# Fused cross-attention and FFN kernel: GpSimd marks the lower limit of the ternary FFN weights, VectorE sums every other load, limits are worked out one load ahead

## The reference

```
def _bitlinear(x, w_latent):
    scale = clip(mean(abs(w_latent), axis=1), 1e-05)        # one per row
    tern = clip(round(w_latent / scale), -1.0, 1.0)
    return x @ (tern * scale).T
h = _bitlinear(x, w_fc) + gate * (x @ v.T @ fast_b.T @ u.T)  # w_fc 2048 x 512
r = relu(h)
return _bitlinear(r * r, w_proj)                             # w_proj 512 x 2048
```

## Time and profile before

| | before |
|---|---|
| median of three runs | 2805.3 us |
| the profiled execution, span | 2803.6 us |
| the profiled execution's own time | not listed apart from the three runs; the median less the span is 1.7 us |
| attention phase | 0 to about 1651 us |
| preparation of the weights | about 1653 to 1724.7 us |
| batch loop of the FFN | 1724.7 us to the end |

### The profile page before, as it was taken

How to read it: one execution, slowest core, us unless ns; L and a number is a source line. 1 busy time by engine, 2 the same in 40 slices (tenths; PEclk the granted TensorE clock), 3 DMA queues, 4 the chain that set the end, 5 groups by cost and what they waited for, 6 DMA issues and landing times. The chain is left out here.

```text
span 2803.6 us, 46166 instructions
## 1 busy us (share of the span) xinstructions
PE 2666.3 (95%) x15410; PEld 1979.3 (71%) x15410; DVE 1688.5 (60%) x3278; ACT 1111.7 (40%) x1965; POOL 377.6 (13%) x791
## 2 busy tenths in 40 slices
PE   7999999999999999999999967999999999999998
PEld 5666666667666666666766645888888888888887
DVE  4676766776767677677676666444444444444444
ACT  2533443443353344244335245444344334433332
POOL 1212121121121212112112110000000000000000
PEclk9999999999999999999999977999999999999999
DMA  4343253333334325333333332000000000000000
GB/s 129 84 112 99 61 135 92 81 98 98 88 85 114 97 62 134 90 79 103 98 85 88 96 104 76 30 30 30 30 30 30 30 30 30 30 30 30 30 30 31
DMA packets 116803, 198.81 MB, mean 71 GB/s; under 512 B 19987, under 2 KB 22035, under 8 KB 116260
## 3 DMA queue, kind: packets, MB, share of 16 engines
q1 hardware_dynamic: 116772, 198.42, 25.6%
HBM read 63.08 MB, written 33.55 MB: 34 GB/s over the span
## 5 line engine op out<-in xcount | busy, mean ns | idle before, releaser
L715 ACT ACTIVATE probs<-bank 128x512 f32<-128x512 f32 x640 | 369.2, 597 | 339.6 <-PE bank L529 329.6
L1125 PE MATMUL y_bank<-projT,a_hi 128*128 128x512 f32 x1024 | 409.1, 399 | 0.0
L1113 PE MATMUL h_bank<-x2T_hi,fcT 128*128 128x512 f32 x1024 | 406.2, 397 | 0.9 <-ACT scale_row L1196 0.9
L1114 PE MATMUL h_bank<-x2T_lo,fcT 128*128 128x512 f32 x1024 | 406.6, 397 | 0.0
L1127 PE MATMUL y_bank<-projT,a_lo 128*128 128x512 f32 x1024 | 403.9, 394 | 0.0
L1204 ACT ACTIVATE relu<-h_bank,scale_fc 128x512 f32<-128x512 f32 x256 | 176.0, 687 | 464.8 <-PE h_bank L1117 464.8
L464 POOL TENSOR_SCALAR_AFFINE_SELECT probs<-probs 128x256 f32<-128x256 f32 (+1 forms) x640 | 234.1, 366 | 872.7 <-ACT probs L715 870.1
L1314 DVE CAST a_hi<-act_sq 128x512 fp32r<-128x512 f32 x256 | 121.0, 472 | 373.6 <-ACT act_sq L1209 373.6
L529 PE MATMUL bank<-stack 98*128 98x512 f32 (+3 forms) x1024 | 286.0, 351 | 28.3 <-ACT probs L715 26.0
L504 PE MATMUL bank<-stack 96*128 96x512 f32 (+3 forms) x1024 | 266.0, 330 | 17.8 <-DVE maxima L777 11.8
L777 DVE TENSOR_REDUCE maxima<-bank 128x1 f32<-128x512 f32 x256 | 175.9, 687 | 162.2 <-PE bank L508 162.2
(11 more groups left out here) (182 smaller groups left out, 4623.9 us busy)
## 6 DMA issues: line engine op xcount, KB each, us to landing
stack<-stage SPq DMA_DIRECT2D x768, 128.0 KB, 2.3
x_in<-in_x_dram SPq DMA_DIRECT2D x16, 1024.0 KB, 5.3
x<-x_res SPq DMA_DIRECT2D x64, 256.0 KB, 2.4
x_in_sb<-x SPq DMA_DIRECT2D x16, 1024.0 KB, 5.6
out_dram<-y_sb SPq DMA_DIRECT2D x64, 256.0 KB, 2.0
xc_rows<-in_ctx_dram SPq DMA_DIRECT2D x15, 1024.0 KB, 5.2
stack<-m_stage SPq DMA_DIRECT2D x128, 8.0 KB, 1.8
w_nat<-in_L_ffn_w_fc_dram SPq DMA_DIRECT2D x2, 1024.0 KB, 6.7
```

The source lines that it names most:

```text
L715: act.activation(probs[:, s[2], :], t_bank[u % 2][:, :], ACT.Exp, scale=SCALE).then_inc(exp_done, 1)
L1113: pe.matmul(h_bank[b % 2][:, :], fcT[:, k, cols], xT_hi[:, k, :], start=k == 0, stop=False)
L1114: pe.matmul(h_bank[b % 2][:, :], fcT[:, k, cols], xT_lo[:, k, :], start=False, stop=False)
L1125: pe.matmul(y_bank[j][:, :], a_hi[:, b % RING, P * j:P * j + P], projT[:, b, :], start=b == 0, stop=False)
```

## The change

- The mark `neg` moves from VectorE to GpSimd, as one `tensor_scalar` per piece, in order of the pieces. It waits for the limits of its load (a new semaphore `limits_ready`) and for `tern` of piece q-2. VectorE's `tern` of a piece waits for its mark (`neg_ready`).
- ScalarE sums the rows of the even loads only. For an odd load VectorE makes the four sums of absolute values in one `tensor_reduce` over 128 x 2048 elements, after waiting for the load itself.
- `SUMS_AHEAD` goes from 6 to 8.
- The thresholds of load n+1 stand between the two pairs of load n, those of load 0 ahead of the loop.

```
+            for q in range(len(PIECES)):            # GpSimd
+                if q % 4 == 0:
+                    pool.wait_ge(limits_ready, q // 4 + 1)
+                if q >= 2:
+                    pool.wait_ge(tern_ready, q - 1)
+                col = q if q < NB else NB + (q - NB) // CHUNKS
+                pool.tensor_scalar(neg[:, q % 2, :], piece_rows(q), neg_half[:, col:col + 1], None, ALU.is_lt
+                                   ).then_inc(neg_ready, 1)
...
             def row_sum(q):                          # ScalarE
+                if q // 4 % 2 == 1:
+                    return
...
                 if q >= 2:
-                    act.wait_ge(sums_ready, q - 1)
+                    act.wait_ge(sums_ready, 4 * (q // 8) + min(q % 8, 4) - 1)
...
             def thresholds(load):                    # VectorE
-                dve.wait_ge(sums_ready, 4 * load + 4)
+                if load % 2 == 0:
+                    dve.wait_ge(sums_ready, 4 * (load // 2) + 4)
+                else:
+                    dve.wait_ge(wn_loaded[load % 3], load // 3 * 16 + 16)
+                    step(dve.tensor_reduce(parts[:, 4 * load:4 * load + 4], w_rows[load % 3][:, :, :], AX.X, ALU.add,
+                                           apply_absolute_value=True))
...
             def ternary(pair):
-                for q in pair:
-                    ...
-                    self_.inc(dve.tensor_scalar(neg[:, q % 2, :], piece_rows(q), neg_half[:, col:col + 1], None,
-                                                ALU.is_lt))
-                dve.wait_ge(dve_self, self_.now())
                 for q in pair:
                     col = q if q < NB else NB + (q - NB) // CHUNKS
+                    dve.wait_ge(neg_ready, q + 1)
                     if q >= 2:
                         dve.wait_ge(tern_full, q - 1)
                     dve.scalar_tensor_tensor(tern[:, q % 2, :], piece_rows(q), half[:, col:col + 1], neg[:, q % 2, :],
                                              ALU.is_gt, ALU.subtract).then_inc(tern_ready, 1)
...
+            thresholds(0)
             for load in range(len(PIECES) // 4):
-                thresholds(load)
                 ternary((4 * load, 4 * load + 1))
+                if load + 1 < len(PIECES) // 4:
+                    thresholds(load + 1)
                 ternary((4 * load + 2, 4 * load + 3))
```

More of the change, by code:

```diff
@@ L933, in ffn_phase @@
         tern_ready = sem("tern_ready")
+        limits_ready = sem("limits_ready")
+        neg_ready = sem("neg_ready")
         tern_full = sem("tern_full")
@@ L962, in ffn_phase @@
         w_rows = (w_nat, y_sb, x_res)
-        SUMS_AHEAD = 6
+        SUMS_AHEAD = 8
         (PREP_GATE_PE, PREP_GATE_ACT, PREP_A_PE, PREP_A_DVE, PREP_A_HIGH_ACT, PREP_A_LOW_DVE, PREP_U_DVE,
@@ L1241, in thresholds @@
                 self_.inc(dve.tensor_scalar(half[:, cols], scale, 0.5, None, ALU.mult))
-                step(dve.tensor_scalar(neg_half[:, cols], scale, -0.5, None, ALU.mult))
+                dve.tensor_scalar(neg_half[:, cols], scale, -0.5, None, ALU.mult).then_inc(limits_ready, 1)
+                dve.wait_ge(dve_self, self_.now())
             def ternary(pair):
@@ L1246, in ternary @@
                     col = q if q < NB else NB + (q - NB) // CHUNKS
-                    if q >= 2:
-                        dve.wait_ge(tern_ready, q - 1)
-                    self_.inc(dve.tensor_scalar(neg[:, q % 2, :], piece_rows(q), neg_half[:, col:col + 1], None,
-                                                ALU.is_lt))
-                dve.wait_ge(dve_self, self_.now())
-                for q in pair:
-                    col = q if q < NB else NB + (q - NB) // CHUNKS
+                    dve.wait_ge(neg_ready, q + 1)
                     if q >= 2:
```

## The result

The changed kernel takes 2819.44 us (median of four runs, 2815.37 to 2822.84) against 2805.41 for the kernel before; the ratio is 1.0043, with a 95% interval from 1.0029 to 1.0057. It is slower by 0.4%, 12 us by the ratio and 14 by the medians. I had forecast 2808.9 us and a range up to 2814.5, so the measured time lies outside. The direction and the place were right, the size was not.

A forecast was written before the change was run, and what follows sets the result against it. VectorE was taken to bound the weights' preparation, whose end moves with the last `tern`. Moved marks, gaps and stalls saved (-14.1 - 0.5 - 2.6) against reductions, waits and new stalls (+8.8 + 8.0 + 4.0) gave +3.6: 2808.9 us, range 2804 to 2814.5.

The forecast's parts named there:

- Where it bounds, and that the end moves with the last `tern`: In the FFN weights' preparation VectorE is busy 45.68 of 49.5 us; the end moves by what the last `tern` moves.
- The select is the nearest in kind ... I add a fifth and take 0.77: Price of a GpSimd mark: a select's 0.64 us at 512 columns plus a fifth for fetched limit and bf16 narrowing.
- Rival 2: Marks take 0.95 us or more and GpSimd's pairs set the pace: +5.6 at 0.95, +11.7 at 1.29; chance 0.26.
- Taking turns: GpSimd's marks and VectorE's `tern` exclude each other: `tern` holds the way for 0.56 us, a mark for 0.67.
- Reductions: VectorE's four sums of odd loads, 128 x 2048 each, cost 2.2 us apiece, 8.8 us in all.
- Sums eight ahead: ScalarE waits for load 4 before piece 16's sum, delaying copies and transposes: VectorE stalls 4.0 us in place of 2.6.
- my walk: Stepping through the 16 pairs, each start the latest of its engine's last start plus slot, its inputs and the turn.
- The sum: All terms for the preparation: -14.1 - 0.5 - 2.6 + 8.8 + 8.0 + 4.0 = +3.6 us.
- waits on marks: VectorE waits for GpSimd's marks, mostly at first pairs of loads and the last pair: 8.0 us in all.
- Rival 1: `tern` does not take turns with marks: -1.0 us with marks at 0.585, 0.0 at 0.77; chance 0.25.
- Rival 3: Denser transposes raise TensorE's clock earlier for the batch loop's first nine matmuls: at most 1.8 us back; chance 0.03.

The follow-up runs named there:

- idle-marks run: Kernel before plus 32 marks on GpSimd that read the layer-norm input into a spare buffer, nobody waiting: preparation 83.1 us, +11.9 against before.
- Order alone: Kernel before with only the sums eight ahead and the limits one load ahead: preparation 73.7 us, +2.4 against before.
- one mark in four: Kernel before, but GpSimd marks only the fourth piece of each load, into one of four slots: preparation 71.6 us, +0.4 against before.
- rounding: Kernel before with mark and `tern` replaced on VectorE by two one-input passes, through rounded int16: preparation 64.3 us, median 2799.31, ratio 0.9977.

## Why the prediction was wrong

*Where it bounds, and that the end moves with the last `tern`:* right. The last `tern` ends at 1733.87 instead of 1720.95, 12.9 later, and the batch loop starts 12.9 later, its matmuls at 397 ns as before.

*"The select is the nearest in kind ... I add a fifth and take 0.77": this is the step that failed.* A mark takes 1.56 us, twice my value and beyond my upper row, the two-input operation at 1.29. I had let the nearest row by kind of work stand for an instruction with another name, and took a two-input operation for an upper bound, which it isn't for another operation. The runs with a constant limit and an fp32 mark show that my two reasons for the fifth, the limit and the narrowing, are worth 0.08 and nothing.

*Rival 2, marks at 0.95 or more:* this is what happened, and it had 0.26. "GpSimd's pairs set the pace" is in the timeline. But its prices ended at 1.29, and the range already at 1.15.

*Taking turns:* right in kind, wrong in its measure. I let a mark hold the way for nearly all its time (0.67 of 0.77). `tern` loses 0.42 when it starts just behind the start of a mark of 1.56 and nothing when it starts 0.7 into one, and x_low and the reduction lose nothing. By my own prices, from 1.0 (+6.3) to 1.29 (+11.7), a mark of 1.56 would have made some +17 (an estimate, that line drawn on); it came to +12.7, so with the right price the sum would have erred the other way. The Trainium skill (SBUF — State Buffer, Who interferes with whom) has the two engines exclude each other. For which operations collide the runs agree: two SBUF inputs (`tern`) and the fast one-input passes (marks, copies) do, one-input reductions and reads of PSUM don't. In another section of that page (SBUF: two separate sides) the Trainium skill has the loser fully blocked for the whole instruction. On this the runs differ: 0.37 us lost per mark of 1.56 in the idle-marks run, where a copy of 0.585 costs 0.27. Had the rule held for the whole instruction, the pace would have been a mark plus the 0.56 that I let a `tern` hold, 2.1 us per piece; while marks set it, it is 1.54.

*Reductions:* 2.2 each, measured 2.27. Right. *Sums eight ahead:* I had ScalarE standing for 4 us in front of the sum of piece 16, and 4.0 us of stalls on VectorE in place of 2.6. ScalarE does stand, for 3.54. What reaches VectorE is less: in the changed kernel it waits 1.16 for TensorE ahead of `tern` 22, where I had 1.9, and under 0.1 ahead of `tern` 14, where I had 2.1; with the marks back on it, 0.7 in all. Order alone costs the 2.4 us of my walk, but by luck, since most of it is the wait for the sums of load 1. This term was too large.

*The sum:* 8.8 for the reductions and 8.0 for waits on marks. The runs put 7.0 us on reductions and order together, where the terms of my sum without marks on GpSimd (a walk with VectorE's own marks) come to 8.2, and 5.7 on the marks. In my 3.6 the marks were thus a gain of 4.6 us; they are a loss of 5.7. That is 10.3 us of error, less the 1.2 by which the rest was put too high: 9.1, the distance from 3.6 to 12.7. The price of a mark makes it: 32 marks and GpSimd's waits are 61.6 us in a row, where VectorE needed 49.5 for everything, and the marks alone are 50 us (32 x 1.56), where mine were 25 (32 x 0.77). No run has a mark at 0.77; the one with 1.48 shows the direction.

*Rival 1, marks are free:* refuted twice, by idle marks that cost 11.9 us and by one mark in four, which gains nothing. *Rival 3, the clock:* granted 0.58 in the stage against 0.60, and the first matmuls of the batch loop again 0.43 apart. It plays no part in the result. It did come in two other kernels, one mark in four and rounding, whose first matmuls of the batch loop are 0.24 apart at once: the loop is 1.5 us shorter there (1077.4 us against 1078.9 before), near the 1.8 of the rival.

What stays open is what GpSimd does in the 1.56 us, why a mark holds VectorE up behind its start and not later, and why a copy costs VectorE 0.27 and a mark 0.37.

## What to carry to other kernels

Before work moves from a full engine to an idle one, price the instruction itself on the idle engine: by a row of the same operation, or by one run with idle copies of it beside the old kernel, which also shows what it costs the engine that it is to relieve. Here a pass of 0.44 us on VectorE became 1.56 on GpSimd and, where it met VectorE's passes, still took about 0.4 of VectorE; none of the schedules tried made it pay. Where one engine is the bound, first look for cheaper forms on that engine (one-input passes and 16-bit data in place of two inputs), and only then give it work to balance the next bound.

## What the runs showed of the hardware that I had not expected

- A compare on GpSimd over 128x512 took 1.56 us with a limit per partition and 1.48 with a constant, more than its two-input add (1.29); its copy takes 0.585.
- A GpSimd instruction that reads SBUF costs VectorE 0.27 us (copy) to 0.44 (mark) when it meets a two-SBUF-input or a fast one-input pass, and nothing beside the 128x2048 reduction (2.27 us with marks, 2.28 without) or a subtraction that reads PSUM (1.28 per pair in both).
- A mark delays a `tern` only by its first part: 0.42 us for one that starts 0.05 behind the mark's start, nothing for one that starts 0.74 into it. A `tern` that starts ahead of the mark keeps its 0.75, and the mark takes longer (1.92 us for one that starts 0.25 behind a `tern`'s start).
- VectorE's int16 to bf16 pass over 128x512 took 0.29 us, its fp32 to int16 pass 0.48, and a write to int16 rounded as the reference's rounding does.
